# Rotary attention: the causal masks of the score maxima as additions on VectorE instead of products on TensorE

## The chip, the core and the metric

The program runs on one core of one Trainium2 chip. The metric is the device time of one execution in microseconds, as the median of the runs shown. One execution was also recorded by the hardware profiler. The engines are named as in the profile: PE is TensorE (matrix products), PEld its loading of weights, DVE is VectorE, ACT is ScalarE, POOL is GpSimd, SP is SyncE, which issues most transfers. PE writes its products to eight banks of the accumulation memory, called `ps[:, bank, :]` in the code.

## The reference, cut to what matters

The reference is a chain of 16 layers over 8 sequences of 512 tokens with 128 features. One of the layers, `L3_attn_a`, is causal attention with 16 heads whose keys and queries have 8 plain and 32 rotary features each:

```
q = concatenate([q_content, q_rope], -1); k = concatenate([k_content, k_rope], -1)
scores = einsum('bhqd,bhkd->bhqk', q, k) / sqrt(40)
causal = tril(ones((Tx, Tx), bool))
scores = where(causal, scores, -inf)
attn = softmax(scores, -1)
out = einsum('bhqk,bhkd->bhqd', attn, v)
return out.reshape(Bx, Tx, 128) @ W_o
```

## The kernel before

The 16 layers run one after the other as stages, each between barriers of all engines. `rotary_attention` is the stage of `L3_attn_a`. It holds every synchronisation by hand: an engine's instructions run in the order of the code, and semaphores tie the engines together.

The stage computes the scores of a sequence twice. First, with queries on the rows, only to get each query's maximum over the keys (below: the maxima). Then, with keys on the rows (the turned scores), with the negated maximum as an additional row of the product, for the exponential on ACT, whose output is multiplied with the values.

*Maxima.* For a head `n` and a tile `qt` of 128 queries the product is 40 features by 128 queries by `(qt + 1) * 128` keys, so 128, 256, 384 or 512 columns wide (line 908). The last 128 columns are the tile on the diagonal: there, keys later than the query are to be masked. `masked` (line 893) does it on PE: two products of 64 rows each, the two halves of a unit matrix times the two halves of a table of 0 and -1e30, both in bf16, add the table to what is in the bank. DVE then takes the maximum of all columns, negated (line 1057), and its end gives the bank back. Heads come in pairs (`pair_of_maxima`), an even and an odd one; the even head's features lie on rows 0 to 39 and its maxima go to bank 6, the odd head's on rows 64 to 103, bank 7. So PE's two row halves can work on the two heads of a pair at once, and there is one bank for each half's maxima.

*Turned scores.* A pass `u` (16 per sequence) takes one key tile `kt = u % 4` of four heads: two steps of two heads, each with a product of `512 - 128 * kt` columns (line 957) and two mask products per head in banks 0 to 3. ACT takes the exponential (line 1035), and the value products (line 973) follow one pass later.

*What sets the order.* The maxima of sequence 0 are taken first, alone: 32 pairs. In the loop over the passes of sequence `b`, each of the two steps of a pass is followed by one pair of maxima of sequence `b + 1`: passes 0, 2, 4, ... have the widths 128 and 256, passes 1, 3, 5, ... the widths 384 and 512. The last sequence's loop has none. After both steps come the value products of the pass before and then `extras`, side items that use banks 6 and 7 as well: the transposes of the maxima (`turn`, line 915), the projections of sequence `b + 2`, rotary products (lines 932 and 934, taken by DVE in lines 1082 and 1083), sums, context and output of sequence `b - 1`. An item on a bank waits until the item before it on that bank has been taken.

The mask table in bf16 is made by POOL (line 873) once the loads have landed; PE, DVE and SP wait for it at the start of the stage.

Of the kernel before, what the change touches and what calls it, by code (L numbers as in the profile page):

```python
# [11 lines left out]
ALU = mybir.AluOpType  # L12
ACT = mybir.ActivationFunctionType
AX = mybir.AxisListType
F32 = mybir.dt.float32

P = 128
START = 1
BATCH = 8
T = 512  # L20
# [231 lines left out]
KT = T // P  # L252
# [449 lines left out]
def rotary_attention(nc, g, w, d, ks, vaug):  # L702
# [7 lines left out]
    tensors = {"qs": ([P, 2, HALVES, T], F32), "negmax": ([P, KT, NH], F32), "maxrow": ([GH, 2, T], F32),  # L710
               "pt": ([P, 2, KT, T], F32), "o": ([P, 2, T], F32), "sel": ([P, 4, P], F32), "sums": ([P, T], F32), "nope": ([P, 2, T], F32), "prod": ([P, 2, 4, T], F32), "rope": ([P, 2, 2, T], F32),
               "wkv": ([P, 32], F32), "gkv": ([32, 1], F32), "wq": ([P, 64], F32), "wkdec": ([32, P], F32), "wqdec": ([64, P], F32), "wvdec": ([32, P], F32), "wkrope": ([P, 4, P], F32),
               "wqrope": ([64, 4, P], F32), "wo": ([P, P], F32), "cos": ([P, T], F32), "sin": ([P, T], F32), "masks": ([P, 2, 3, P], F32), "masksb": ([P, 2, 3, P], BF16),
               "kvc": ([32, 2, T], F32), "kvsq": ([32, T], F32), "qc": ([64, T], F32), "mean32": ([32, P], F32)}
    loads = [("sel", "sel")] + [(a, "L3a_" + a) for a in ("wkv", "gkv", "wq", "wkdec", "wqdec", "wvdec", "wkrope", "wqrope", "wo", "cos", "sin", "masks")]

# [63 lines left out]
    for item in order():  # L780
# [2 lines left out]
        used[bank] += 1  # L783

    signals = ("loaded pool_ready ready6 ready7 taken6 taken7 squared rooted scaled rope_made nope_written rope_written0 rope_written1 first_stacked second_stacked max_written "
               "max_stacked turned_ready exp_ready pv_done o_copied pool vec")
    with stage(nc, "L3a", tensors, signals) as (block, t, s):
        h, x, ps = g["h"], g["x"], g["ps"]
        nope_d, rope_d, row_d = d["nope"], d["rope"], d["row"]
# [4 lines left out]
        def ready(eng, item):  # L794
            bank, k = place[item]
            eng.wait_ge(s[f"ready{bank}"], START + k + 1)
            return ps[:, bank, :]
# [70 lines left out]
        @block.gpsimd  # L868
        def _(pool):
            own = Chain(pool, s["pool"])  # L870
            own(pool.memset(t["mean32"][:, :], 1.0 / 32))
            pool.wait_ge(s["loaded"], START + LOADED)
            own(pool.tensor_copy(t["masksb"][:, :, :, :], t["masks"][:, :, :, :]), s["pool_ready"], 1)
            for b in range(BATCH):
                for k in range(4):
                    part, half = divmod(k, 2)
                    for ab in range(2):
                        taken(pool, ("rope", b, part, half, ab))

                    pool.wait_ge(s[f"rope_written{k % 2}"], START + (2 * b + k // 2) * 16)  # L880
                    prod = t["prod"][:, k % 2, :, :]
                    pool.tensor_tensor(t["rope"][:, k % 2, 0, :], prod[:, 0, :], prod[:, 3, :], ALU.subtract).then_inc(s["rope_made"], 1)
                    pool.tensor_tensor(t["rope"][:, k % 2, 1, :], prod[:, 2, :], prod[:, 1, :], ALU.add).then_inc(s["rope_made"], 1)

        @block.tensor
        def _(pe):
# [9 lines left out]
            def side(item):  # L896

                bank, k = place[item]
                pe.wait_ge(s[f"taken{bank}"], START + k)
                what, b = item[:2]  # L900
                out = ps[:, bank, :]
                tokens = h[:, b * T:(b + 1) * T]
                if what == "max":
                    n, qt = item[2:]
                    if n % GH == 0 and qt == 0:
                        pe.wait_ge(s["second_stacked" if n else "first_stacked"], START + (b + 1) * STACKED)
                    rows = row_tile(n % 2, KEYED)
                    pe.matmul(out[:, 0:(qt + 1) * P], t["qs"][rows, b % 2, n // 2, qt * P:(qt + 1) * P], ks[rows, b % 2, n // 2, 0:(qt + 1) * P], start=True, stop=False)  # L908
                    mm = masked(out[:, qt * P:(qt + 1) * P], n % 2, 1)
                elif what == "turn":  # L910
                    k = item[2]
                    for r in range(2):
                        taken(pe, ("max", b, GH * k + GH - 2 + r, KT - 1))
                    for qt in range(KT):
                        mm = pe.transpose(out[0:GH, qt * P:(qt + 1) * P], t["negmax"][:, qt, GH * k:GH * (k + 1)], g["ident"][:, :])
                elif what == "kv":
                    mm = pe.matmul(out[0:32, :], t["wkv"][:, :], tokens, start=True, stop=True)
                elif what == "qc":
                    mm = pe.matmul(out[0:64, :], t["wq"][:, :], tokens, start=True, stop=True)
                elif what == "rms":  # L920
                    pe.wait_ge(s["squared"], START + b + 1)
                    mm = pe.matmul(out, t["mean32"][:, :], t["kvsq"][:, :], start=True, stop=True)
                elif what == "qn":
                    taken(pe, ("qc", b))
                    mm = pe.matmul(out, t["wqdec"][:, :], t["qc"][:, :], start=True, stop=True)
                elif what == "kn":
                    pe.wait_ge(s["scaled"], START + b + 1)
                    mm = pe.matmul(out, t["wkdec"][:, :], t["kvc"][:, b % 2, :], start=True, stop=True)
                elif what == "rope":
                    part, half, ab = item[2:]  # L930
                    if part:
                        mm = pe.matmul(out, t["wqrope"][:, 2 * half + ab, :], t["qc"][:, :], start=True, stop=True)
                    else:
                        mm = pe.matmul(out, t["wkrope"][:, 2 * half + ab, :], tokens, start=True, stop=True)
                elif what == "v":
                    pe.wait_ge(s["scaled"], START + b + 1)
                    for kt in range(KT):
                        cols = slice(kt * P, (kt + 1) * P)
                        mm = pe.matmul(out[:, cols], t["kvc"][:, b % 2, cols], t["wvdec"][:, :], start=True, stop=True)
                elif what in ("sums", "ctx"):  # L940
                    pe.wait_ge(s["o_copied"], START + 2 * b + 2)
                    for e in range(2):
                        mm = pe.matmul(out, t["sel"][:, (2 if what == "sums" else 0) + e, :], t["o"][:, e, :], start=(e == 0), stop=(e == 1))
                else:
                    taken(pe, ("ctx", b))
                    mm = pe.matmul(out, t["wo"][:, :], t["sums"][:, :], start=True, stop=True)
                mm.then_inc(s[f"ready{bank}"], 1)
# [97 lines left out]
        def _(vec):  # L1045
# [4 lines left out]
            def maxima(b, i):  # L1050

                for item in pair_of_maxima(b, i):
                    n, qt = item[2:]
                    out = ready(vec, item)
                    if qt == 0 and n % GH == 0 and b:
                        ready(vec, ("turn", b - 1, n // GH))
                    taken_by(vec.tensor_reduce(t["negmax"][:, qt, n:n + 1], out[:, 0:(qt + 1) * P], AX.X, ALU.max, negate=True), item)  # L1057

            def take(item):
# [2651 lines left out]
```

## Time and profile before

| | |
|---|---|
| median of 3 runs | 7737.04 us (7718.37 to 7741.0) |
| profiled execution | 7739.17 us, span 7737.4 us |
| granted clock of PE over the span | 0.83 |
| PE busy | 5852.5 us, 76% of the span |
| DVE busy | 4148.7 us, 54% |
| ACT busy | 2938.2 us, 38% |
| POOL busy | 1964.7 us, 25% |
| rotary stage | about 4131 to 5085 us from the span's start |

Busy time is time in which the engine worked on an instruction; the ends of PE's products are modelled, so a busy PE is not a PE at its peak. The granted clock is the share of PE's full clock that it was given. A product on 32-bit data appears as two records.

### The profile page before, as it was taken

To read this page: it belongs to the slowest core of one execution; us is meant where nothing else is said; L and a number is where in the kernel's file an instruction comes from. 1 tells how busy PE (TensorE), PEld (TensorE's weight loads), DVE (VectorE), ACT (ScalarE), POOL (GpSimd) and SP (SyncE) were. 2 spreads that over 40 slices of the span, in tenths; PEclk is the share of its full clock that TensorE was granted. 3 is DMA by queue.
4 is the path that set the end of the run, shared out by engine and by line. 5 is a ranking of instruction groups with operands and counts; after the bars stand their busy time and mean duration, and the time that the engine had idled before them with its cause. 6 is when DMAs were issued, how large, how long until landed. Compare 5 with 4: busy or idle time off the path is not lost. (4 is left out here: it accounts for less than half of the span.)

```text
span 7737.4 us, 121045 instructions
## 1 busy us (share of the span) xinstructions
PE 5852.5 (76%) x45636; PEld 2850.6 (37%) x45838; DVE 4148.7 (54%) x6437; ACT 2938.2 (38%) x6433; POOL 1964.7 (25%) x1790
## 2 busy tenths in 40 slices
PE   5556667786578876666568999978878889688787
PEld 3445351115352222222223545534434334244343
DVE  4333636662437745778854444445455466555554
ACT  1002223463235541443310222246546455365464
POOL 0004142113142201444422001024234011242341
PEclk6557887897788888787787787889989989899898
DMA  1001022212121100000003122111011000110110
GB/s 46 4 28 56 30 62 75 66 42 69 50 66 39 39 17 14 0 0 0 0 7 62 38 49 54 29 43 45 20 53 45 9 6 0 39 45 23 53 45 20
DMA packets 261164, 269.01 MB, mean 35 GB/s; under 512 B 113600, under 2 KB 190656, under 8 KB 258688
## 3 DMA queue, kind: packets, MB, share of 16 engines
q1 hardware_dynamic: 250368, 240.26, 12.0%
q0 software_dynamic: 10240, 21.25, 0.8%
q8 instruction: 359, 5.88, 0.3%
q14 instruction: 197, 1.61, 0.1%
HBM read 122.59 MB, written 71.66 MB: 25 GB/s over the span
## 5 line engine op out<-in xcount | busy, mean ns | idle before, releaser
L2250 PE MATMUL ps<-s_l2b_hc,ident 128*128 128x512 f32 x512 | 362.4, 848 | 331.0 <-DVE s_l2b_hc L2413 331.0
L2198 POOL TENSOR_TENSOR s_l2b_Bx<-s_l2b_du,s_l2b_B 128x512 f32<-128x512 f32 x256 | 406.5, 1609 | 473.9 <-ACT s_l2b_B L2320 410.8
L1827 PE MATMUL ps<-s_l3l_hs,s_l3l_wqk 128*128 128x512 f32 x512 | 330.9, 754 | 223.5 <-DVE s_l3l_prod L1978 156.5
L1954 ACT ACTIVATE s_l3l_probs<-ps,s_l3l_biases,s_l3l_q_inverse 128x128 f32<-128x128 f32 x1024 | 454.1, 458 | 58.1 <-DVE s_l3l_biases L2024 57.8
L2405 DVE TENSOR_TENSOR_SCAN s_l2b_state<-s_l2b_decay,s_l2b_Bx 128x512 f32<-128x512 f32 x256 | 389.8, 1562 | 155.2 <-ACT s_l2b_decay L2326 113.9
L2022 DVE TENSOR_REDUCE s_l3l_negmax<-ps 128x4 f32<-128x512 f32 x256 | 176.5, 690 | 524.3 <-PE ps L1866 524.3
L1057 DVE TENSOR_REDUCE s_L3a_negmax<-ps 128x1 f32<-128x128 f32 (+3 forms) x512 | 236.3, 488 | 362.9 <-PE ps L893 360.6
L1802 POOL TENSOR_TENSOR s_l3l_probs<-s_l3l_probs,s_l3l_inverse 128x512 f32<-128x512 f32 x256 | 266.6, 1042 | 635.4 <-DVE s_l3l_inverse L2004 633.0
L1035 ACT ACTIVATE s_L3a_pt<-ps 128x256 f32<-128x256 f32 (+3 forms) x512 | 195.2, 434 | 529.3 <-PE ps L893 527.5
L638 DVE TENSOR_REDUCE s_L1a_negmax<-ps 128x1 f32<-128x512 f32 x512 | 316.4, 682 | 139.7 <-PE ps L501 139.3
L908 PE MATMUL ps<-ks,s_L3a_qs 40*128 40x256 f32 (+3 forms) x1024 | 359.8, 610 | 31.3 <-DVE s_L3a_kvsq L1072 16.5
L638 DVE TENSOR_REDUCE s_L2a_negmax<-ps 128x1 f32<-128x512 f32 x512 | 316.7, 682 | 92.1 <-PE ps L501 91.2
L614 ACT ACTIVATE s_L1a_pt<-ps 128x512 f32<-128x512 f32 x512 | 263.1, 603 | 199.2 <-PE ps L537 199.1
L614 ACT ACTIVATE s_L2a_pt<-ps 128x512 f32<-128x512 f32 x512 | 263.3, 604 | 167.0 <-PE ps L537 166.8
L1866 PE MATMUL ps<-s_l3l_qk 64*64 64x64 f32 (+1 forms) x5632 | 281.9, 247 | 42.6 <-issue 24.6
L2250 PEld LDWEIGHTS ps<-s_l2b_hc,ident 128*128 128x128 f32 x512 | 122.0, 257 | 488.9 <-DVE s_l2b_hc L2413 428.6
L957 PE MATMUL ps<-s_L3a_qs,ks 41*128 41x512 f32 (+3 forms) x1024 | 284.2, 567 | 0.1
L1866 PEld LDWEIGHTS ps<-s_l3l_qk 64*64 64x64 f32 x5632 | 218.8, 138 | 161.1 <-issue 161.1
L1948 ACT ACTIVATE s_l3l_turned<-ps 128x512 f32<-128x512 f32 x256 | 152.9, 597 | 316.5 <-PE ps L1874 315.7
L1925 ACT ACTIVATE s_l3l_sq<-ps 128x512 f32<-128x512 f32 x256 | 150.1, 601 | 263.6 <-PE ps L1827 263.6
L501 PE MATMUL ps<-ks,s_L2a_qs 48*128 48x512 bf16 x512 | 177.6, 438 | 85.2 <-DVE s_L2a_negmax L638 37.5
L501 PE MATMUL ps<-ks,s_L1a_qs 48*128 48x512 bf16 x512 | 179.1, 450 | 83.0 <-DMA ks<-scratch_parts 34.7
(663 smaller groups left out, 13292.4 us busy)
## 6 DMA issues: line engine op xcount, KB each, us to landing
s_l3l_qk<-s_l3l_rope SPq DMA_DIRECT2D x1024, 64.0 KB
scratch_rope<-s_L3a_rope SPq DMA_DIRECT2D x32, 512.0 KB, 2.8
ks<-scratch_parts SPq DMA_DIRECT2D x384, 32.0 KB
s_L3a_qs<-scratch_rope SPq DMA_DIRECT2D x64, 128.0 KB
ks<-scratch_rope SPq DMA_DIRECT2D x64, 128.0 KB
s_L0e_slots<-scratch_sent SPq DMA_DIRECT2D x16, 396.0 KB, 5.6
s_L1e_slots<-scratch_sent SPq DMA_DIRECT2D x16, 396.0 KB, 6.0
scratch_square<-s_L1a_rows SPq DMA_DIRECT2D x24, 256.0 KB, 3.0
```

Source lines behind the costliest of these rows:

```text
L501: mm = pe.matmul(out, t["qs"][rows, b % 2, n // 2, qt * P:(qt + 1) * P], ks[rows, b % 2, n // 2, :], start=True, stop=True)
L614: act.activation(t["pt"][:, u % 2, j, :], ps[:, j, :], ACT.Exp, scale=scale).then_inc(s["exp_ready"], 1)
L638: taken_by(vec.tensor_reduce(t["negmax"][:, qt, n:n + 1], out, AX.X, ALU.max, negate=True), item)
L908: pe.matmul(out[:, 0:(qt + 1) * P], t["qs"][rows, b % 2, n // 2, qt * P:(qt + 1) * P], ks[rows, b % 2, n // 2, 0:(qt + 1) * P], start=True ...
L957: pe.matmul(ps[:, 2 * pair + r, first(kt):T], ks[rows, b % 2, 2 * four + pair, kt * P:(kt + 1) * P], t["qs"][rows, b % 2, 2 * four + pair, ...
L1802: own(pool.tensor_tensor(tile, tile, share, ALU.mult), s["probs_ready"], U + 1)
L1827: mm = pe.matmul(out, t["wqk"][:, 2 * e + ab, :], tokens, start=True, stop=True)
L1866: mm = pe.matmul(out[rows, P * k + at:P * k + at + size], t["qk"][rows, b % 2, c, 64 * m:64 * m + 64], t["qk"][rows, b % 2, 4 + c, key:key ...
L1954: act.activation(t["probs"][:, U % (LAG + 1), k, :], ps[:, U % 2, P * k:P * (k + 1)], ACT.Exp, bias=t["biases"][:, U % (LAG + 1), k:k + 1] ...
L2198: pool.tensor_tensor(t["Bx"][:, n % 2, k, :], t["du"][:, b % 2, k, :], t["B"][:, n % 2, :], ALU.mult).then_inc(s["bx_ready"], 1)
L2250: pe.matmul(ps[:, 4 + k, :], g["ident"][:, :], t["hc"][:, n % 2, k, :], start=(n == 0), stop=(n == STATES - 1)).then_inc(s["summed"], 1)
L2405: vec.tensor_tensor_scan(t["state"][:, k, :], t["decay"][:, n % 2, k, :], t["Bx"][:, n % 2, k, :], 0.0, ALU.mult, ALU.add).then_inc(s["sca ...
```

## The change

The two mask products of each head's maxima are left out; the score product alone fills the bank. DVE instead adds a mask tile of 128 by 128 in 32 bits to the last 128 columns, in the bank, waits for that addition with a semaphore of its own (`masked`), and then takes the maximum as before. The tile is made on POOL at the start of the stage by a fill and a cut along the diagonal. The turned scores keep their mask products.

```diff
-               ... "masksb": ([P, 2, 3, P], BF16),
+               ... "masksb": ([P, 2, 3, P], BF16), "mask": ([P, P], F32),
...
             own(pool.memset(t["mean32"][:, :], 1.0 / 32))
+            own(pool.memset(t["mask"][:, :], 0.0))
+            own(pool.affine_select(out=t["mask"][:, :], in_=t["mask"][:, :], compare_op=ALU.is_ge, fill=-1e30, base=0, pattern=[[-1, P]], channel_multiplier=1))
             pool.wait_ge(s["loaded"], START + LOADED)
...
                     rows = row_tile(n % 2, KEYED)
-                    pe.matmul(out[:, 0:(qt + 1) * P], t["qs"][rows, b % 2, n // 2, qt * P:(qt + 1) * P], ks[rows, b % 2, n // 2, 0:(qt + 1) * P], start=True, stop=False)
-                    mm = masked(out[:, qt * P:(qt + 1) * P], n % 2, 1)
+                    mm = pe.matmul(out[:, 0:(qt + 1) * P], t["qs"][rows, b % 2, n // 2, qt * P:(qt + 1) * P], ks[rows, b % 2, n // 2, 0:(qt + 1) * P], start=True, stop=True)
...
                         ready(vec, ("turn", b - 1, n // GH))
+                    last = out[:, qt * P:(qt + 1) * P]
+                    vec.tensor_tensor(last, last, t["mask"][:, :], ALU.add).then_inc(s["masked"], 1)
+                    vec.wait_ge(s["masked"], START + NH * KT * b + 2 * i + n % 2 + 1)
                     taken_by(vec.tensor_reduce(t["negmax"][:, qt, n:n + 1], out[:, 0:(qt + 1) * P], AX.X, ALU.max, negate=True), item)
```

On PE, an odd pass with 128-wide turned scores read thus before; each row is an instruction with its output and inputs and the size of its output, `xN` is how often it stands there:

```order
L957 MATMUL ps<-s_L3a_qs,ks 128x128 x2
L893 MATMUL ps<-s_L3a_masksb 128x128 x4
L908 MATMUL ps<-ks,s_L3a_qs 128x384
L893 MATMUL ps<-s_L3a_masksb 128x128 x2
L908 MATMUL ps<-ks,s_L3a_qs 128x384
L893 MATMUL ps<-s_L3a_masksb 128x128 x2
L957 MATMUL ps<-s_L3a_qs,ks 128x128 x2
L893 MATMUL ps<-s_L3a_masksb 128x128 x4
L908 MATMUL ps<-ks,s_L3a_qs 128x512
L893 MATMUL ps<-s_L3a_masksb 128x128 x2
L908 MATMUL ps<-ks,s_L3a_qs 128x512
L893 MATMUL ps<-s_L3a_masksb 128x128 x2
```

The same pass of the changed kernel, whose lines have other numbers (957 is 958, 893 is 895, 908 is 910):

```order
L958 MATMUL ps<-s_L3a_qs,ks 128x128 x2
L895 MATMUL ps<-s_L3a_masksb 128x128 x4
L910 MATMUL ps<-ks,s_L3a_qs 128x384 x2
L958 MATMUL ps<-s_L3a_qs,ks 128x128 x2
L895 MATMUL ps<-s_L3a_masksb 128x128 x4
L910 MATMUL ps<-ks,s_L3a_qs 128x512 x2
```

The two heads' products now follow each other directly, and only the turned scores' mask products remain. On DVE, between the copy of the values and the reciprocal of the sums (pass 4), four reduces stood before:

```order
L1088 COPY vaug<-ps 128x64x8
L1057 TENSOR_REDUCE s_L3a_negmax<-ps 128x1 x4
L1093 RECIPROCAL s_L3a_sums<-ps 128x512
L1097 TENSOR_TENSOR s_L3a_sums<-s_L3a_sums,ps 128x512
L1057 TENSOR_REDUCE s_L3a_negmax<-ps 128x1 x8
```

Now, in the changed kernel:

```order
L1092 COPY vaug<-ps 128x64x8
L1059 TENSOR_TENSOR ps<-ps,s_L3a_mask 128x128
L1061 TENSOR_REDUCE s_L3a_negmax<-ps 128x1
L1059 TENSOR_TENSOR ps<-ps,s_L3a_mask 128x128
L1061 TENSOR_REDUCE s_L3a_negmax<-ps 128x1
L1059 TENSOR_TENSOR ps<-ps,s_L3a_mask 128x128
L1061 TENSOR_REDUCE s_L3a_negmax<-ps 128x1
L1059 TENSOR_TENSOR ps<-ps,s_L3a_mask 128x128
L1061 TENSOR_REDUCE s_L3a_negmax<-ps 128x1
L1097 RECIPROCAL s_L3a_sums<-ps 128x512
```

Each reduce has an addition ahead of it, even head and odd head in turn, and the reciprocal stands behind four of each.

## Rows read from the trace of the kernel before

**Rows 1.** The page, its first line: the span.

```profile
span 7737.4 us, 121045 instructions
```

**Rows 2.** Windows of the stage: length, busy PE PEld DVE ACT POOL, PEclk, DMA share, GB/s.

```profile
4192.00:4267.00 75.00, 72.74 (x260) 42.94 (x262) 33.38 (x69) 1.87 (x2) 6.25 (x6) 0.52 0.42 78
4267.00:4376.00 109.00, 105.21 (x693) 57.88 (x691) 47.37 (x88) 31.03 (x73) 9.97 (x8) 0.77 0.17 39
4598.80:4710.30 111.50, 106.29 (x716) 55.44 (x716) 52.11 (x92) 31.35 (x75) 9.96 (x8) 0.83 0.26 51
```

**Rows 3.** Waits in the stage, 4185 to 5100 us: total us, times, longest.

```profile
DVE s_L3a_negmax L1057 <- PE ps L893: 360.6, 294, 4.7
PEld ps L893 <- issue: 159.6, 485, 0.7
...
PEld ps L915 <- DVE s_L3a_negmax L1057: 15.3, 14, 1.7
PEld ps L908 <- DVE s_L3a_negmax L1057: 15.3, 62, 0.5
```

**Rows 4.** Timeline of PE in three places: start, length, instruction, [idle before <- releaser].

```profile
4430.70 0.29 PE L893 MATMUL ps<-s_L3a_masksb 64*128 64x128 bf16 x4
4430.81 0.66 PE L957 MATMUL ps<-s_L3a_qs,ks 41*128 41x256 f32 x4
4431.30 0.29 PE L893 MATMUL ps<-s_L3a_masksb 64*128 64x128 bf16 x4
4431.41 0.84 PE L908 MATMUL ps<-ks,s_L3a_qs 40*128 40x256 f32 x4
...
4688.76 0.48 PE L893 MATMUL ps<-s_L3a_masksb 64*128 64x128 bf16 x4
4688.97 2.08 PE L957 MATMUL ps<-s_L3a_qs,ks 41*128 41x512 f32 x4
4690.78 0.48 PE L893 MATMUL ps<-s_L3a_masksb 64*128 64x128 bf16 x4
...
4707.35 0.33 PE L893 MATMUL ps<-s_L3a_masksb 64*128 64x128 bf16 x4
4707.89 1.16 PE L908 MATMUL ps<-ks,s_L3a_qs 40*128 40x512 f32 x3 [0.21 <-DVE s_L3a_negmax L1057]
```

**Rows 5.** Timeline of DVE in three places.

```profile
4431.01 0.49 DVE L1057 TENSOR_REDUCE s_L3a_negmax<-ps 128x1 f32<-128x128 f32 x2 [2.64 <-PE ps L893]
...
4610.96 0.68 DVE L1067 COPY s_L3a_kvc<-ps 32x512 f32<-32x512 f32 x1 [1.68 <-PE ps L917]
4611.68 0.68 DVE L1069 TENSOR_TENSOR s_L3a_kvsq<-s_L3a_kvc 32x512 f32<-32x512 f32 x1
...
4707.27 1.02 DVE L1057 TENSOR_REDUCE s_L3a_negmax<-ps 128x1 f32<-128x384 f32 x2 [1.56 <-PE ps L893]
```

**Rows 6.** One group of the stage: count, busy us, mean ns, idle before.

```profile
L893 PE MATMUL ps<-s_L3a_masksb 64*128 64x128 bf16 x2048 | 233.2, 248 | 0.0
```

**Rows 7.** Single lines of other stages: duration in ns, least, median, most.

```profile
L2767 DVE TENSOR_TENSOR s_L1e_steps<-s_L1e_prefix,s_L1e_steps x2: 293/293/293, 1801.7 to 2091.9; 128x128 f32<-128x128 f32 x2
...
L2496 DVE TENSOR_TENSOR s_L2r_hot<-s_L2r_hot,s_L2r_order x4: 424/425/426, 2868.9 to 3992.0; 128x256 f32<-128x256 f32 x4
...
L1368 DVE TENSOR_TENSOR s_l0a_NT<-ps,s_l0a_masks x16: 424/424/425, 102.8 to 464.4; 128x256 f32<-128x256 f32 x16
```

**Rows 8.** Timeline in the first maxima, a 512-wide pair: PE, then DVE.

```profile
4258.17 1.16 PE L893 MATMUL ps<-s_L3a_masksb 64*128 64x128 bf16 x4
4258.63 1.43 DVE L1057 TENSOR_REDUCE s_L3a_negmax<-ps 128x1 f32<-128x512 f32 x2 [1.64 <-PE ps L893]
```

**Rows 9.** Timeline of POOL at the start of the stage.

```profile
4141.59 0.82 POOL L873 CAST s_L3a_masksb<-s_L3a_masks 128x768 bf16<-128x768 f32 x1 [9.96 <-DMA s_L3a_masks<-in_L3a_masks_dram]
```

**Rows 10.** Passes 11 to 14 of sequences 6 and 5, columns as in rows 2.

```profile
4913.71:4930.77 17.06, 16.88 (x160) 9.59 (x161) 8.37 (x18) 5.98 (x16) 2.48 (x2) 1.00 0.51 92
4789.14:4817.74 28.60, 28.43 (x161) 14.35 (x161) 8.36 (x18) 5.97 (x16) 2.49 (x2) 0.55 0.41 66
```

More of the change, by code:

```diff
@@ L712, in rotary_attention @@
                "wkv": ([P, 32], F32), "gkv": ([32, 1], F32), "wq": ([P, 64], F32), "wkdec": ([32, P], F32), "wqdec": ([64, P], F32), "wvdec": ([32, P], F32), "wkrope": ([P, 4, P], F32),
-               "wqrope": ([64, 4, P], F32), "wo": ([P, P], F32), "cos": ([P, T], F32), "sin": ([P, T], F32), "masks": ([P, 2, 3, P], F32), "masksb": ([P, 2, 3, P], BF16),
+               "wqrope": ([64, 4, P], F32), "wo": ([P, P], F32), "cos": ([P, T], F32), "sin": ([P, T], F32), "masks": ([P, 2, 3, P], F32), "masksb": ([P, 2, 3, P], BF16), "mask": ([P, P], F32),
                "kvc": ([32, 2, T], F32), "kvsq": ([32, T], F32), "qc": ([64, T], F32), "mean32": ([32, P], F32)}
@@ L785, in rotary_attention @@
     signals = ("loaded pool_ready ready6 ready7 taken6 taken7 squared rooted scaled rope_made nope_written rope_written0 rope_written1 first_stacked second_stacked max_written "
-               "max_stacked turned_ready exp_ready pv_done o_copied pool vec")
+               "max_stacked masked turned_ready exp_ready pv_done o_copied pool vec")
     with stage(nc, "L3a", tensors, signals) as (block, t, s):
```

## The prediction

> **What bounds the kernel now.** I read the views from the whole to the place. The page gives the span [rows 1]. The windows of the rotary stage come next [rows 2]: in every stretch TensorE (PE) is busy for about 96% of the time and VectorE (DVE) for under half, so PE looks like the bound; the column PEclk says that it gets 0.52 of its full clock while the maxima of sequence 0 are taken alone, 0.77 to 0.83 in the loops over passes. Its clock has two levels, 1.2 and 2.4 GHz, so 0.83 is two thirds of the time at the upper one. Then the waits [rows 3]: DVE waits 360.6 us in all for the products of the maxima. The other direction is small, 15.3 us in 62 waits of PE's weight loads for the reduce. It is small because PE's two row halves (even head, odd head) overlap: while one waits, the other counts as busy. Whether DVE already sets the pace must be read from the timeline, pair by pair.
>
> There [rows 4, 5], upper clock, pass 2 of a sequence: the masks of a pair start at 4430.70 and the next scores at 4430.81, so four mask products hold PE 0.11 us. The two reduces start at 4431.01, 0.31 us after the masks, and last 0.49 us together, until 4431.50. The second pair of maxima begins at 4431.41: its even head fits in, its odd head needs the bank that is free only at 4431.50. So here there is no slack between DVE and PE at all. In pass 15 it is plainer: the scores' masks begin at 4707.35, yet the next pair starts at 4707.89 after an idle 0.21 us that the row puts down to the reduce; the first of the two 384-wide reduces (1.02 us for both, from 4707.27) ends at about 4707.8. At the lower clock mask products hold PE 0.21 us (4688.76 to 4688.97), and the 512-wide scores behind them 1.81 us (to 4690.78): there PE is slow enough that DVE is mostly done in time.
>
> So of the four second pairs in four passes, three are released by DVE at the upper clock; the first pairs come after value products and a new pass's scores, and DVE was idle before them, 2.64 us ahead of the reduces of 4431.01. That is where the additions land.
>
> **The change part by part.** *Removed from PE:* four of the eight mask products per score-and-maxima step. In the loops there are 7 sequences of 32 pairs, 224 pairs. Two thirds at 0.11 and one third at 0.21 us [rows 4] give 224 x 0.145 = 33 us. This is the lower end of the gain: all 2048 mask products together are busy 233.2 us [rows 6], of which half, 117 us, is the upper end. I take 33, because the start-to-start times show what PE really gives up and the busy time counts pipelined ends.
>
> *Added to DVE:* per head one addition of 128 columns and a wait on itself. The trace has no addition that writes a bank. The nearest row is 128x128 in SBUF, 0.293 us; at 256 columns an addition or product with an operand in the bank takes 0.424 us and one all in SBUF 0.425 us [rows 7], so the bank costs nothing extra when read, and I take 0.293. The self-wait costs 0.04 us: the copy of line 1067 starts at 4610.96 and lasts 0.68, the instruction that waits for it starts at 4611.68 [rows 5]. Together D = 0.33 us per head. Bounds: below, 0.21 us, what a second 128-wide reduce adds to its row (0.49 for two, the first 0.28); above, 0.424 + 0.04 = 0.46 us.
>
> The Trainium skill, Perfetto Trace Analysis, section Optimizing Scalar/DVE Operations, speaks against this choice: it gives DVE an access overhead of about 60 ns on SBUF and 125 ns on PSUM, the latency in a profile being about twice that. By it an addition in the bank would take some 0.42 us as an estimate, D 0.46, and the sum below 30 us more; the rows on bank operands do not agree for reads, and no row shows a write.
>
> *Where D falls on the path.* The odd head's bank is released after two additions and two reduces, 2D = 0.66 us later when both heads are ready together, D when the odd head is itself late by more than D. PE's own part is earlier by the masks, which is counted already. Of each second pair there are 28 (7 sequences, 4 four-pass groups), 19 at the upper clock by two thirds.
> - Scores 256 wide between (passes 2, 6, ...): no slack at the upper clock, 19 x 0.66; at the lower the scores take twice as long, 0.4 us of slack, 9 x 0.27. Sum 15 us.
> - Scores 512 wide between (passes 0, 4, ...): at the upper clock they last 0.42 us more than 256-wide ones (0.90, half of 1.81, against the 0.49 from 4430.81 to the masks of 4431.30), less the 0.14 by which the odd head is late above: slack 0.28, 19 x 0.38 = 7 us. Nothing at the lower clock.
> - The 512-wide maxima of odd passes (384- or 128-wide scores ahead): released by DVE now, as in pass 15; 0.66 where the heads are in step, 0.33 where the odd one is late. I take 0.5 for all 56: 28 us.
>
> Together 50 us of waits. *Behind them:* what is queued behind the waiting reduce on DVE are the side items' products and copies, and the side items on PE need the same two banks. The transposes of the maxima wait for the reduce 14 times already [rows 3]; those, the sums of pass 4 and two rotary products per sequence find little slack. Some 20 starts later by D: 6 us.
>
> *The first maxima* (sequence 0, lower clock) are a chain per bank: product, masks, reduce, next product [rows 8], the reduce 0.46 us after the masks began. Each of 32 items per bank loses 0.21 of masks and gains 0.33: 32 x 0.12 = 4 us.
>
> *GpSimd* fills and cuts the mask tile, two instructions on 128 columns, in the 9.96 us in which it waits for the masks' load; its cast of 768 columns behind that takes 0.82 us [rows 9], so the two cost nothing, and without that cover at most 2 x 0.82 us.
>
> Sum with the clock as it is: 50 + 6 + 4 - 33 = +27 us.
>
> *The clock.* The same four passes (11 to 14) took 17.06 us at a granted 1.00 in sequence 6 and 28.60 us at 0.55 in sequence 5 [rows 10]: about 2.9 us per pass at the lower level. In the first stretch of rows 2, where PE alternates with DVE, the clock stayed low, in the loops it is high two thirds of the time. After the change PE has fewer columns and longer waits, so the same direction. I take five more low passes of 112, +15 us; this is a choice, bounded by nothing worse than rival 1 and by 0 on the other side.
>
> Forecast +42 us. The profiled execution took 7739.17 us (span 7737.4), 2 us over the median of the three runs, 7737.04; so 7737 + 42, 7779 us, with 7760 to 7815 as its own range.
>
> **The rivals.**
> 1. *The clock falls for much longer.* If one more group of four passes per sequence runs low, 7 x 11.5 = 80 us on top of 27: about 7845 us. For it: the first maxima ran low throughout. Against: at the lower clock the waits on DVE vanish and PE is dense again, after which it rose each time. The Trainium skill, TensorE: Matmul & The Clock Gate, section on a second failure mode (cycling through PSUM banks), says that short idle times between matmul groups make the clock swing; the trace agrees in so far as the clock changes in these loops, and by that rule this rival is the outcome.
> 2. *No change.* If the addition costs its lower bound, D 0.21, the same three terms give 8 + 3 + 17 = 28 us, behind them 4, the first maxima 0, the masks -33: 7736 us. For it: in a queue without waits the end of one DVE instruction overlaps the start of the next. Against: this addition is waited for by the very next instruction.
> 3. *Faster.* The mask products cost PE more than their start-to-start time, since each also needs its weights loaded. At the upper end of 117 us the sum is 50 + 6 + 4 - 117 = -57: 7680 us. The point from which it decides is 0.27 us saved per pair (60 over 224). For it: 159.6 us of idle on the load path ahead of mask loads [rows 3]. Against: in the rows the next matmul starts 0.11 us after the masks, no later.
>
> **How the numbers follow.** Measurable from no change is here about 0.3%, 23 us. Forecast 0.47, rival 1 0.18, rival 2 0.20, rival 3 0.15. So faster 0.15, same 0.20, slower 0.65. The range takes in rival 2, most of rival 1 and the part of rival 3 that a saving of some 0.35 us per pair would give, 7718; left out are its far end and a clock low in most passes, together under 2 in 10: 7718 to 7845.
>
> **What would show it.** Right: the additions take 0.27 to 0.32 us and the reduce follows 0.04 us later; the waits of PE's weight loads for the reduce of the maxima, 15.3 us before [rows 3], grow several fold; the stage lengthens by 30 to 60 us, and outside it nothing moves by more than a few. The 256-wide second pairs start their odd head about 0.5 us later after the even one. Wrong: additions under 0.25 us, a second pair that starts right behind the scores, or a granted clock in the loops that moves by over 0.05 either way, which outweighs the waits.

## The result and the profile after

The changed kernel takes 7815.62 us (median of 4 runs, 7810.0 to 7830.81); the kernel before 7732.91 (median of 4, 7718.37 to 7741.0). The ratio is 1.0112, 95% interval 1.0096 to 1.0127: slower by about 83 us. The forecast was slower by 42 us, 7779, with a range to 7845. The direction and the range held; the size is twice the forecast, and it has to be found where the other half came from. The profiled execution took 7810.0 us, that of the kernel before 7739.17. Each trace is one execution, so the traces differ by 71 us where the medians differ by 83. On its page the span answers to [rows 1]:

```profile
span 7808.3 us, 119513 instructions
## 1 busy us (share of the span) xinstructions
PE 5921.6 (76%) x44612; PEld 2817.6 (36%) x44814; DVE 4295.0 (55%) x6949; ACT 2940.3 (38%) x6433; POOL 1964.3 (25%) x1792
```

The additions are one line of DVE. The view of that line gives their duration (least, median, most, in ns), and the timeline of DVE shows them in a pass of the same kind as in the first part of [rows 5], at the upper clock:

```profile
L1059 DVE TENSOR_TENSOR ps<-ps,s_L3a_mask x512: 287/299/300, 4205.4 to 5108.3; 128x128 f32<-128x128 f32 x171
```

```profile
5017.62 0.30 DVE L1059 TENSOR_TENSOR ps<-ps,s_L3a_mask 128x128 f32<-128x128 f32 x1 [2.46 <-PE ps L910]
5017.95 0.29 DVE L1061 TENSOR_REDUCE s_L3a_negmax<-ps 128x1 f32<-128x128 f32 x1
5018.16 0.29 DVE L1059 TENSOR_TENSOR ps<-ps,s_L3a_mask 128x128 f32<-128x128 f32 x1
5018.48 0.29 DVE L1061 TENSOR_REDUCE s_L3a_negmax<-ps 128x1 f32<-128x128 f32 x1
```

An addition lasts 0.30 us and its reduce starts 0.03 us behind it. So the even head's bank is free at 5018.24 and the odd head's at 5018.77, and the next product of PE waits for each: the two heads' products start at 5018.30 and 5018.83, 0.53 us apart. The waits of the stage, 4185 to 5170 us, in rows that answer to [rows 3] (lines 908, 915, 1057 of before are 910, 916, 1061 here):

```profile
DVE ps L1059 <- PE ps L910: 276.4, 248, 4.3
...
PEld ps L895 <- issue: 92.1, 215, 0.7
...
PEld ps L910 <- DVE s_L3a_negmax L1061: 79.9, 150, 1.9
...
PEld ps L916 <- DVE s_L3a_negmax L1061: 22.2, 15, 2.8
```

The weight loads of the maxima (line 908, now 910) waited 15.3 us in 62 waits for the reduces and now wait 79.9 us in 150.

Where the time went is read from windows with equal marks: a pass begins with its first product of maxima. First the kernel before, in the columns of [rows 2]: the whole stage; sequences 1 to 6 of the loops; then sequence 4 in its pieces (passes 0 and 1, 2 to 4, 5 to 10, 11 to 14, 15); last, one pass with 256-wide scores and no side item at the upper and at the lower clock.

```profile
4131.40:5080.50 949.10, 886.03 (x5536) 458.37 (x5536) 406.00 (x711) 244.66 (x581) 80.68 (x66) 0.77 0.24 48
4269.32:4937.41 668.09, 636.10 (x4147) 332.29 (x4144) 299.04 (x531) 187.95 (x440) 59.77 (x48) 0.80 0.24 47
4602.27:4612.51 10.24, 10.24 (x86) 5.46 (x81) 4.92 (x10) 5.04 (x10) 0.00 (x0) 1.00 0.75 91
4612.51:4641.86 29.35, 25.86 (x147) 13.90 (x141) 12.93 (x16) 8.97 (x19) 0.00 (x0) 0.71 0.03 10
4641.86:4680.05 38.19, 36.85 (x265) 18.99 (x265) 21.40 (x41) 10.28 (x27) 7.48 (x6) 1.00 0.13 49
4680.05:4706.26 26.21, 26.04 (x160) 13.14 (x161) 8.36 (x18) 5.97 (x16) 2.49 (x2) 0.61 0.46 72
4706.26:4711.39 5.13, 4.92 (x55) 2.74 (x50) 3.00 (x5) 0.89 (x4) 0.00 (x0) 1.00 0.35 79
4927.68:4930.77 3.09, 3.09 (x46) 2.17 (x41) 1.25 (x4) 1.32 (x4) 0.00 (x0) 1.00 1.09 102
4812.21:4817.74 5.53, 5.53 (x45) 3.53 (x41) 1.24 (x4) 1.32 (x4) 0.00 (x0) 0.50 0.00 1
```

The same windows of the changed kernel, with the first maxima as the second row:

```profile
4140.90:5163.50 1022.60, 951.65 (x4512) 427.85 (x4512) 556.19 (x1224) 244.78 (x581) 81.11 (x68) 0.71 0.22 44
4204.35:4282.33 77.98, 73.72 (x138) 33.29 (x140) 50.32 (x130) 1.87 (x2) 4.93 (x4) 0.50 0.40 72
4282.33:5003.35 721.02, 685.11 (x3380) 312.31 (x3378) 412.19 (x916) 186.92 (x438) 59.71 (x48) 0.73 0.22 44
4645.06:4660.78 15.72, 15.72 (x68) 7.52 (x65) 7.31 (x18) 5.04 (x10) 0.00 (x0) 0.58 0.34 42
4660.78:4691.36 30.58, 28.19 (x123) 13.19 (x117) 16.53 (x28) 8.46 (x18) 0.00 (x0) 0.61 0.03 10
4691.36:4730.95 39.59, 37.35 (x217) 16.81 (x217) 28.23 (x65) 10.81 (x28) 7.47 (x6) 1.00 0.13 47
4730.95:4757.10 26.15, 25.70 (x128) 11.10 (x130) 13.14 (x34) 5.97 (x16) 2.48 (x2) 0.61 0.43 72
4757.10:4764.48 7.38, 6.74 (x47) 2.81 (x42) 4.24 (x9) 0.89 (x4) 0.00 (x0) 0.74 0.55 104
5017.14:5020.68 3.54, 3.47 (x39) 2.06 (x34) 2.44 (x8) 1.32 (x4) 0.00 (x0) 1.00 0.04 8
5097.33:5102.71 5.38, 5.38 (x37) 3.07 (x34) 2.44 (x8) 1.31 (x4) 0.00 (x0) 0.50 0.00 0
```

Read them in this order. The stage is 73.5 us longer, while the span grew by 70.9. Outside the stage the code is the same, and there the traces differ both ways: the stage starts 9.5 us later and the part behind it is 12.1 us shorter. Over all traces of this case the stage starts between 4120 and 4145 us, so some ten us outside the stage are no effect of the change. Of the stage's 73.5 us sequences 1 to 6 hold 52.9, everything from the maxima of sequence 7 to the end of the stage 17.1 (143.1 to 160.2 us), the first maxima 3.4 (74.6 to 78.0); ahead of them the stage took 63.4 and 63.5 us. Within sequence 4, passes 5 to 10 ran at 1.00 both times and cost 1.40 us more; passes 11 to 14 ran at 0.61 both times and cost 0.06 less. Ten of sixteen passes together: +1.3 us. Passes 0 and 1, whose clock went from 1.00 to 0.58, cost 5.48 more, and pass 15, from 1.00 to 0.74, 2.25 more. So three passes whose clock changed hold 7.7 of the sequence's 10.3 us, and passes 2 to 4, at 0.71 before and 0.61 now, 1.2. The pattern repeats: sequences 3 to 6 of the changed kernel take 119.41, 119.42, 119.43 and 119.44 us, with nearly the same clocks in the same passes. So a pass that is pushed to the lower clock can cost its price once in every sequence.

### The profile page after: what moved, and what is told of

It is laid out like the page before. It is cut to its first block and busy times, and to the rows that moved or that the text cites. A ratio compares the mean times of both kernels' runs of the same rounds, so it can differ in the third digit from the quotient of the medians.

```text
span 7808.3 us, 119513 instructions
## 1 busy us (share of the span) xinstructions
PE 5921.6 (76%) x44612; PEld 2817.6 (36%) x44814; DVE 4295.0 (55%) x6949; ACT 2940.3 (38%) x6433; POOL 1964.3 (25%) x1792
## 5 line engine op out<-in xcount | busy, mean ns | idle before, releaser
L910 PE MATMUL ps<-ks,s_L3a_qs 40*128 40x128 f32 (+3 forms) x1024 | 408.5, 661 | 35.0 <-DVE s_L3a_kvsq L1076 13.0
L1059 DVE TENSOR_TENSOR ps<-ps,s_L3a_mask 128x128 f32<-128x128 f32 x512 | 151.4, 296 | 279.8 <-PE ps L910 276.4
L958 PE MATMUL ps<-s_L3a_qs,ks 41*128 41x512 f32 (+3 forms) x1024 | 302.7, 615 | 0.0
L501 PE MATMUL ps<-ks,s_L1a_qs 48*128 48x512 bf16 x512 | 182.0, 457 | 80.6 <-DMA ks<-scratch_parts 33.7
```

Source lines behind the costliest of these rows:

```text
L910: mm = pe.matmul(out[:, 0:(qt + 1) * P], t["qs"][rows, b % 2, n // 2, qt * P:(qt + 1) * P], ks[rows, b % 2, n // 2, 0:(qt + 1) * P], start ...
L958: pe.matmul(ps[:, 2 * pair + r, first(kt):T], ks[rows, b % 2, 2 * four + pair, kt * P:(kt + 1) * P], t["qs"][rows, b % 2, 2 * four + pair, ...
```

## The experiments

**The two theories.** The theory of the sum: the loss is waits of PE for the additions, less the mask products. The theory of the clock: most of it is the granted clock of PE, which falls in other places than before. The expectations of the first runs split it in two: by the waits theory the clock follows PE's waits for DVE, by the columns theory it follows how many products PE has. Loops are sequences 1 to 6, from the first maxima product of sequence 1 to that of sequence 7; the kernel before is 668.1 us at 0.80, the changed one 721.0 at 0.73. The kernels ran in three groups; the kernel before took 7726.13, 7722.23 and 7733.01 us in them (medians of 17, 17 and 18 runs), and each ratio is against its own group.

**Masks on neither engine, and on both.** These two and the two kernels of the case make a square: mask products of the maxima or none, additions or none. The first run leaves the masks of the maxima out (its exponent is scaled down so that it stays finite, and its output is not the layer's):

```diff
-                    last = out[:, qt * P:(qt + 1) * P]
-                    vec.tensor_tensor(last, last, t["mask"][:, :], ALU.add).then_inc(s["masked"], 1)
-                    vec.wait_ge(s["masked"], START + NH * KT * b + 2 * i + n % 2 + 1)
...
```

> The maxima get no mask at all, neither on PE nor on DVE, and the exponent is scaled down by 1000 so that no sum vanishes; the output is therefore not the layer's. It prices the removal of 1024 mask products alone. Waits theory (the clock fell in the changed kernel because PE waits longer for DVE): no added wait, so the clock in the loops stays at 0.78 to 0.83 and the 33 us of the loops and 7 us of the first maxima come off: about 7690 us. Columns theory (the clock fell because PE has four products fewer per step): the clock falls to about 0.74 here too, and the time is 7720 to 7745 us.

The second puts the mask products of the maxima back beside the additions:

```diff
-  mm = pe.matmul(out[:, 0:(qt + 1) * P], ..., start=True, stop=True)
+  pe.matmul(out[:, 0:(qt + 1) * P], ..., start=True, stop=False)
+  mm = masked(out[:, qt * P:(qt + 1) * P], n % 2, 1)
```

> The changed kernel with the mask products of the maxima put back, so that each mask is added twice, by PE and by DVE. PE has all products of before, DVE all additions of after. Waits theory: the clock falls as in the changed kernel, loops at about 0.74, and the time is that of after plus the 33 us and 7 us of mask products: 7845 to 7860 us. Columns theory: the clock is that of before, 0.82, and only the waits of 50 + 6 and 11 us in the first maxima are added: about 7800 us.

Without masks 7723.65 us, ratio 0.9998 (0.9985 to 1.0011); with both 7879.71, ratio 1.0196 (1.0182 to 1.0211). Windows of the loops and of the pass kind shown last above, upper clock, then lower, first for the kernel without masks, then for the one with both:

```profile
4269.61:4945.58 675.97, 639.38 (x3379) 292.22 (x3377) 298.28 (x531) 187.02 (x438) 59.73 (x48) 0.75 0.23 47
5013.92:5016.78 2.86, 2.86 (x38) 1.75 (x34) 1.24 (x4) 1.32 (x4) 0.00 (x0) 1.00 0.00 0
4813.41:4818.35 4.94, 4.94 (x37) 2.63 (x34) 1.24 (x4) 1.32 (x4) 0.00 (x0) 0.50 0.05 7
```

```profile
4292.75:5067.98 775.23, 741.10 (x4149) 380.16 (x4145) 412.70 (x916) 186.96 (x438) 59.80 (x48) 0.70 0.20 41
5108.02:5111.78 3.76, 3.70 (x46) 2.42 (x41) 2.44 (x8) 1.32 (x4) 0.00 (x0) 1.00 0.00 0
4926.83:4932.63 5.80, 5.80 (x45) 3.77 (x41) 2.44 (x8) 1.32 (x4) 0.00 (x0) 0.50 0.00 1
```

At one clock level the pass is a sum, plain at the upper level and to within 0.17 us at the lower. Upper level: the additions cost 0.67 us with masks (3.09 to 3.76) and 0.68 without (2.86 to 3.54); the mask products cost 0.23 without additions and 0.22 with them. Lower level: additions 0.27 with masks (5.53 to 5.80) and 0.44 without; masks 0.59 and 0.42. The whole is no such sum. Taking the masks away saves nothing where there are no additions (0.9998) and about 0.85% where there are (1.0196 against 1.0112). The kernel without masks is faster than the one before at both levels, yet its loops are 8 us longer, because the clock gave 0.75 instead of 0.80. That is the theory of the clock, in a kernel that has no added instruction at all. It doesn't have unchanged waits, though: without the mask products PE comes to the banks earlier and waits longer for the same reduces, 43.4 us in 92 waits against 15.3 in 62 [rows 3]:

```profile
PEld ps L908 <- DVE s_L3a_negmax L1056: 43.4, 92, 1.6
```

So the first run, whose time and clock are about those that the columns theory gave, doesn't separate missing columns from longer waits. The second came out above both forecasts, at 0.70 with all products of before; by the columns theory its clock would have stayed.

**One half of the additions.** Tiles 0 and 2 are the first pairs of a pass, tiles 1 and 3 the second ones; the other half keeps its mask products.

```diff
+                    if qt % 2 == 0:        # second run: == 1
                         last = out[:, qt * P:(qt + 1) * P]
...
```

> DVE adds the mask only for the first pair of each pass (query tiles 0 and 2); the second pair (tiles 1 and 3) keeps its mask products. My steps: the release of the first pair's banks is what the second pair waits for, so nearly all 50 us of waits are here, with half of the mask saving, 16 us. Waits theory: clock about 0.75 in the loops, 7800 to 7830 us. Columns theory: half the columns are gone, clock between, about 7780 us.

> The other half: DVE adds the mask only for the second pair of each pass (tiles 1 and 3), whose banks are needed only a pass later; the first pair keeps its mask products. My steps: nearly no wait but the side items' 6 us, half of the mask saving, 16 us: 7715 to 7735 us, clock as before. Columns theory: the same columns are gone as in the run on the first pairs, so the same clock as there, about 7760 to 7780 us.

First pairs: 7830.76 us, ratio 1.0144 (1.0129 to 1.0158), loops 740.6 us at 0.72. Second pairs: 7766.49, ratio 1.0047 (1.0033 to 1.006). At one clock the additions that hurt are those of a first pair, since the second pair of its pass waits for the banks; behind a second pair come value products and a new pass, with time to spare. Passes 5 to 10 show it, at the upper clock throughout: 38.19 us before, 39.74 with additions on first pairs, 38.00 on second pairs. Windows: these passes in sequence 2 of the first run; then of the second run its loops, the same passes in sequence 3, and the pass kind that took 3.09 us before, upper clock:

```profile
4440.10:4479.84 39.74, 37.91 (x241) 18.57 (x241) 24.90 (x53) 10.79 (x28) 7.47 (x6) 1.00 0.13 47
```

```profile
4269.52:4989.59 720.07, 688.99 (x3765) 332.28 (x3761) 354.00 (x724) 186.88 (x438) 59.73 (x48) 0.72 0.21 44
4555.53:4593.53 38.00, 36.31 (x240) 17.49 (x241) 24.65 (x53) 10.24 (x27) 7.47 (x6) 1.00 0.13 49
5055.73:5058.71 2.98, 2.98 (x42) 1.95 (x37) 1.72 (x6) 1.32 (x4) 0.00 (x0) 1.00 0.00 0
```

On second pairs the pass is 0.11 us shorter than before, the loops 52 us longer, at 0.72: in the loops the loss is nearly all clock. (The rest of its stage ran at 0.99 and gave part back.) The expectation of 7715 to 7735 us missed by over 30: its sum held in passes 5 to 10, but not its clock. The time and the clock, the same 0.72 as on first pairs, are those of the columns theory; on first pairs the time was within 1 us of the range of the waits theory. Neither theory fits all four runs.

**Giving PE work back.** If the missing columns lowered the clock, more of them should raise it; so says the density theory of the expectations, by which waits and missing products both lower the clock. Three kernels: the changed one with each mask product of the turned scores done twice; the changed one with the 128-wide turned scores done three times and the 256-wide ones twice, in the wait ahead of the second pair; the kernel before with the 128-wide ones done twice.

```diff
-                for j in range(2):
+                for j in range(4):                                           # the first
+  again = (0, 0, 1, 2)[kt] if pair and b + 1 < BATCH else 0                  # the second; (0, 0, 0, 1) the third
+  for k in range(again + 1):
       for r in range(2):
...
```

> The changed kernel with the turned scores' mask products done twice (the masked scores only become more negative): PE has as many products as before, but none of the added ones between the maxima and DVE. Density theory (the clock falls both when PE waits and when it has fewer products): PE is denser than in after, the clock in the loops rises from 0.73 to 0.76 or more, which gives back part of the 40 us that the products cost: 7815 to 7845 us. Rival (the clock follows the waits alone): 0.72 or less and 7855 us or more.

> The changed kernel with products that change nothing put where PE waits for DVE: ahead of the second pair of maxima the turned score product is done two more times where it is 128 wide and once more where it is 256 wide (the last one counts). Density theory: they run in time that was idle, PE stays denser and the clock in the loops rises to 0.78 or more: 7770 to 7800 us, faster than after with more work. Rival (only the waits for DVE count, the clock is a symptom): not faster than 7810 us, and up to 7840 us if the products do not fit into the waits.

> The kernel before with the same filler in its one plain wait: ahead of the second pair of maxima the 128-wide turned score product is done once more. Density theory: clock in the loops 0.82 or more instead of 0.80, 7700 to 7720 us, faster than before. Rival: the work adds to the path or is hidden, 7727 to 7740 us.

7809.87 us (ratio 1.0115, 1.0099 to 1.0131), 7792.82 (1.0096, 1.0081 to 1.0111) and 7722.41 (1.0006, 0.9995 to 1.0016). The first has 768 matmuls more in its loops than the changed kernel and takes the same time (1.0115 against 1.0112, 5 us under the forecast range), its loops 708.8 us at 0.77: there the work is paid by a higher clock. The other two don't bear the theory out. The second has a time in the forecast range, but its loops ran at 0.73, not at the 0.78 expected, and took 727.4 us; its interval overlaps that of the changed kernel. The third ran at 0.79 in loops of 675.5 us, against 0.80 and 668.1, and is as fast as the kernel before, where 0.82 or more and a gain were expected. So one of three fillers raised the clock, and neither of the two for the changed kernel brings it near the one before.

**One addition for both heads.** 256 columns, after both products, then the two reduces:

```diff
+                last = ps[:, 6:8, qt * P:(qt + 1) * P]
+                vec.tensor_tensor(last, last, both, ALU.add).then_inc(s["masked"], 1)
...
```

> The changed kernel with one addition of 2 x 128 columns for both heads of a pair (about 0.42 us, as the 256-wide rows) in place of two of 0.296 with a wait each. The odd head's bank comes free 0.2 us earlier, the even one's 0.13 us later. By my steps the waits of the second pairs shrink by about 0.2 us each where the heads are in step: 10 to 15 us at the same clock, 7800 to 7806 us; if the clock follows the waits it rises by 0.01 to 0.02 and another 10 to 20 us come off: 7780 to 7795 us. Rival (the odd head's release is not what the loops wait for): 7815 us or more.

7953.95 us, ratio 1.0301 (1.0286 to 1.0316): the expectation missed by some 150 us. The view of the line, then windows of the first maxima, of the loops, and of the known pass kind at the upper and at the lower clock:

```profile
L1061 DVE TENSOR_TENSOR ps<-ps,s_L3a_mask x256: 431/433/433, 4198.6 to 5258.2; 128x256 f32<-128x256 f32 x128
```

```profile
4196.47:4293.55 97.08, 61.08 (x138) 30.00 (x140) 42.87 (x98) 1.87 (x2) 4.93 (x4) 0.50 0.32 58
4293.55:5145.78 852.23, 795.04 (x3379) 360.65 (x3377) 379.37 (x724) 187.21 (x438) 59.71 (x48) 0.59 0.19 37
5189.92:5193.71 3.79, 3.42 (x38) 2.04 (x33) 2.22 (x7) 1.32 (x4) 0.00 (x0) 1.00 0.00 0
5247.43:5252.72 5.29, 5.29 (x37) 2.83 (x34) 2.11 (x6) 1.32 (x4) 0.00 (x0) 0.50 0.00 0
```

DVE is indeed busy for less (379 against 412 us in the loops). But now the even head waits for the odd one, no product of the next pair starts before both, and the pass takes 3.79 instead of 3.54 us at the upper clock; at the lower one it takes 5.29 instead of 5.38. In the first maxima, low in both kernels, the lock costs 19 us (97.1 against 78.0). In the loops 0.25 us for each of 96 passes would be 24 us; they lost 131, at a clock of 0.59. An estimate from these rows: 852.23 us at 0.59 and 721.02 at 0.73 are about 699 and 389 us at the lower level, and 310 us more there, at 5.29 for 3.79, cost some 88. So most of this loss too came with the clock. The expectation reckoned with the addition alone.

**One wait, in one place.** Ahead of the products of the maxima no wait of PE itself for a reduce is longer, in the changed kernel, than the 0.64 us in pass 15, where it waited 0.21 us before [rows 4]; in sequence 4 the clock falls about 1.6 us after that row begins, and stays low until pass 1 of the next sequence. Timeline of PE:

```profile
4758.95 2.08 PE L910 MATMUL ps<-ks,s_L3a_qs 40*128 40x512 f32 x4 [0.64 <-DVE s_L3a_negmax L1061]
```

Is it this wait that makes it fall? Four kernels choose the engine by a rule; the first is the changed kernel with pass 15's 384-wide maxima masked by PE, the second its mirror, the third has all 384-wide maxima on PE, the fourth is a control with the 14 additions in pass 7:

```diff
+    def added(b, n, qt):
+        return b == 0 or n < NH - 2 or qt != 2         # 1
+        return b > 0 and n >= NH - 2 and qt == 2       # 2
+        return qt != 2                                 # 3
+        return b > 0 and n // 2 == 3 and qt == 2       # 4
...
```

> The changed kernel, with only the 384-wide maxima of pass 15 of each looped sequence masked by TensorE as before (56 of 512 additions fewer... exactly 14: two heads, seven sequences). In the changed kernel TensorE stands idle 0.64 us there (before 0.21), and the granted clock falls about 1.6 us later and stays low until pass 1 of the next sequence. Theory A, that this one wait makes it fall: passes 15, 0 and 1 run at the upper level again in most sequences, the loops of sequences 1 to 6 come from 721 us to 675 to 695, the whole to 7765 to 7790 us. Theory B, that the clock answers to all waits and to the missing mask products together, or falls elsewhere: within 6 us of the changed kernel, 7805 to 7820 us.

> The mirror of the run above: every mask by TensorE as in the kernel before, and the addition on VectorE only for the 384-wide maxima of pass 15 of each looped sequence, 14 additions in all. At the same clock it costs at most 7 x 0.45 us, 3 us. Theory A (this wait makes the clock fall for passes 15 to 1): 7745 to 7775 us. Theory B (no single wait does it): 7722 to 7735 us, no difference that can be measured.

> The changed kernel, with all 384-wide maxima (query tile 2, the first pair of every odd pass) masked by TensorE, the other three tiles by additions on VectorE. The waits of the 512-wide second pairs in odd passes go back to those of the kernel before, so that at the same clock the loops lose about 15 us against the changed kernel. Theory A (the long waits ahead of the 512-wide maxima make the clock fall): 7740 to 7775 us. Theory B (the clock answers to all of it): 7780 to 7805 us.

> A control for the run with additions in pass 15 alone: the same 14 additions, but on the 384-wide maxima of pass 7, in a stretch (passes 5 to 10) where both kernels keep the upper clock. Theory A (the place decides, pass 15 is on the edge): 7722 to 7735 us, no difference. Theory B (no single wait does it): the same. A third theory, that any one wait more makes the clock fall: 7745 to 7775 us.

Windows of the first: its loops, passes 0 and 1 of sequences 4 and 5.

```profile
4271.47:4996.97 725.50, 693.40 (x3405) 316.31 (x3402) 408.49 (x904) 186.90 (x438) 59.74 (x48) 0.72 0.21 43
4640.93:4656.69 15.76, 15.76 (x68) 7.55 (x65) 7.31 (x18) 5.04 (x10) 0.00 (x0) 0.58 0.43 43
4758.04:4769.01 10.97, 10.71 (x70) 4.73 (x65) 7.64 (x19) 5.04 (x10) 0.00 (x0) 1.00 0.76 89
```

It takes 7815.94 us (ratio 1.0107, 1.0085 to 1.0129), as the changed kernel does: theory B of its expectation. (The count in it is 14 additions, two heads in seven sequences.) The wait is back at 0.20 us, and in sequences 5 and 7 passes 0 and 1 do run at the upper clock, but then passes 6 and 7 or others run low: the low stretch moved. Theory A, that this one wait sets the changed kernel's time, is refuted. The row of sequence 5 also prices the change in passes 0 and 1 at one clock: 10.97 against 10.24 us.

The mirror takes 7767.72 us, ratio 1.0052 (1.0032 to 1.0071), 35 us for 14 additions. Its trace is its fastest execution, 7744.35 us. Windows: loops, pass 15 of sequence 4, passes 0 and 1 behind it.

```profile
4267.62:4958.00 690.38, 657.09 (x4123) 336.61 (x4120) 303.30 (x543) 186.91 (x438) 59.81 (x48) 0.77 0.23 46
4721.74:4729.13 7.39, 6.75 (x51) 3.11 (x45) 3.70 (x7) 0.89 (x4) 0.00 (x0) 0.75 0.59 100
4729.13:4745.37 16.24, 16.24 (x85) 7.66 (x81) 4.92 (x10) 5.05 (x10) 0.00 (x0) 0.59 0.37 38
```

Here theory A's range holds: the clock falls in pass 15 and passes 0 and 1 cost 16.24 instead of 10.24 us. But in sequences 3 and 5 of the same trace pass 15 ran at 1.00, and the passes 0 and 1 behind it were low all the same (16.33 and 16.37 us at 0.58). So the range is borne out and theory A's path only in part. The third kernel takes 7801.49 us, ratio 1.0078 (1.0054 to 1.0102), in theory B's range; its loops, expected to be some 15 us shorter than those of the changed kernel at the same clock, are 14 us longer, 734.6 us at 0.70. The control takes 7714.01 us, ratio 0.9975 (0.9964 to 0.9987), which none of its three theories had. Its windows, as for the mirror:

```profile
4270.80:4931.32 660.52, 629.86 (x4123) 329.49 (x4120) 302.45 (x543) 186.99 (x438) 59.75 (x48) 0.81 0.24 48
4707.78:4712.90 5.12, 4.92 (x55) 2.73 (x49) 3.00 (x5) 0.89 (x4) 0.00 (x0) 1.00 0.33 75
4712.90:4723.14 10.24, 10.24 (x86) 5.47 (x81) 4.91 (x10) 5.04 (x10) 0.00 (x0) 1.00 0.84 94
```

In its trace every sequence from the second on takes 109.1 to 109.2 us, with passes 0 and 1 at 1.00, where those of the kernel before took 109, 111 or 115. So the same 14 additions cost 35 us in one pass and gain 19 in another. Of the runs here it is the one that beats both kernels, by 0.25%, less than the 0.3% that the prediction took as measurable, though the interval leaves 1 out. Why a wait in pass 7 keeps the clock in step is not settled, so it is no recipe.

## Why the prediction was right or wrong

**The price of an addition: right.** 0.296 us as a mean and 0.03 to the reduce, D = 0.33 as taken from [rows 5, 7]; an addition in the bank takes no longer than the SBUF row of 0.293. The estimate worked out from the Trainium skill, Perfetto Trace Analysis, section Optimizing Scalar/DVE Operations, 0.42 us, does not hold in this trace: the longest of 512 additions took 0.300 us.

**Where D falls: right.** For a second pair behind 256-wide scores the sum said 0.66 us at the upper and 0.27 at the lower clock; the square measured 0.67 and 0.68, and 0.27 (0.44 without mask products). Eight mask products in a pass, 0.22 and 0.42 by [rows 4], were 0.22 to 0.23 and 0.42 to 0.59. So the pass should lose 0.44 at the upper clock and gain 0.15 at the lower, and it lost 0.45 (3.09 to 3.54) and gained 0.15 (5.53 to 5.38). The heads' products start 0.53 us apart, where the prediction had about 0.5. For odd passes the sum was too high: 0.5 of waits less 0.22 of masks is 0.28 us a pass, and passes 5 and 7 of sequence 4, at 1.00 in both traces, grew by 0.11 each (6.43 to 6.54 and 7.60 to 7.71).

**The first maxima: right.** 4 us, measured 3.4. GpSimd's share at nothing is right: from the start of the stage to the first maxima the traces take 63.4 and 63.5 us. The waits of PE's loads grew fivefold, as said.

**The sum at one clock, +27 us: right within what can be told.** In sequence 4, 1.40 (passes 5 to 10) and -0.06 (11 to 14) are measured at equal clocks, and so is 0.73 for passes 0 and 1, with the run that masked pass 15 on PE; for passes 2 to 4 and 15 I estimate 1 us from the 0.45 of the one pass kind. That is about 3 us for a sequence, 21 for seven, 24 with the first maxima.

**The clock: the term that was too small.** The prediction took "five more low passes of 112, +15 us; this is a choice". Its direction was right. By the line above, 73.5 - 24, about 50 us of the stage are the clock's, more than three times as much. An estimate by another way agrees: by its rows, 949.10 us at 0.77 and 1022.60 at 0.71, the stage spent about 437 and then 593 us at the lower level, some 157 more; the known pass kind takes 5.38 us there and 3.54 at the upper level, so 157 us there cost some 54. Passes 0 and 1 ran wholly at the upper clock in sequences 3, 4 and 5 before and in none after; passes 11 to 14 of sequence 6 did so before, 17.06 us [rows 10], and took 26.19 us at 0.61 after. This is the mechanism of rival 1, which had one more group of four passes low in every sequence, 80 us and 7845 in all; the result lies between, at 7816, and nearer to the rival than to the forecast. It is at the end of the forecast's own range (7815); the full range held because most of rival 1 was taken in. The prediction also named, as a sign that it was wrong, a clock in the loops that moves by more than 0.05 and outweighs the waits: it moved by 0.07. And the stage grew by 73.5 us, not by 30 to 60. The reason against rival 1, that at the lower clock PE is dense and the clock comes back, says nothing on when it falls again.

**What moves the clock.** Shown: it fell when additions came with the same PE work (0.80 to 0.70), and when mask products went and nothing was added (0.80 to 0.75). In the second case PE's waits for the reduces grew as well, 15.3 to 43.4 us. The Trainium skill, TensorE: Matmul & The Clock Gate, section A second HAM failure mode, names short idle times between groups of matmuls as what makes the clock swing; the growth of the waits in the kernel without masks agrees with it. Not shown is whether missing products alone, at unchanged waits, lower the clock. Not shown either is where it will fall: a wait in pass 15 goes with a lower clock in one kernel and, taken out of another, only moves the fall. That cause stays open.

**Rivals 2 and 3.** An addition at the lower bound is refuted by its row. That masks cost more than their start-to-start time is true by a little at the lower clock (0.59 against 0.42 where no addition is made). Per pair that is 0.11 us at the upper clock and 0.21 to 0.30 at the lower, and the rival needed 0.27 on average. In the whole time the kernel without any mask shows that even all of them, with no addition in their place, returned nothing.

## What to carry to other kernels

Where TensorE's granted clock is a mix of its two levels, price a change pass by pass at each level, and keep the clock as a term of its own, as wide as the passes near the edge between the levels; here it was some 50 of the 73.5 us by which the stage grew. Work taken from TensorE in such a loop may give nothing back, and a gain in a pass can end as a loss: with additions on second pairs alone passes 5 to 10 were 0.19 us shorter at the upper clock, and the whole was 0.47% longer. So a change is to be read in the whole time and not in a pass. When one of two alternating pairs has slack behind it, additional work costs less there: at the upper clock additions on second pairs did not lengthen passes 5 to 10, those on first pairs did, by 1.55 us.

## What the runs showed that was not expected

- Fourteen additions, 4 us of DVE's time in all, changed the whole by +35 us in pass 15 and by -19 us in pass 7.
- 768 more matmuls in the loops (the mask products of the turned scores twice) left the time as it was, 7809.87 against 7815.62 us (ratios 1.0115 and 1.0112), at a clock of 0.77 instead of 0.73.
- The kernel without masks has 768 matmuls less in its loops than the kernel before (3379 against 4147) and takes the same time, 7723.65 against 7726.13 us.
- An addition of 256 columns in the bank took 0.433 us against 2 x 0.296 for two of 128, and the kernel with it lost some 140 us against the one with two. It ties the two heads together, which cost 19 us in the first maxima at one clock; most of the rest came with a clock of 0.59 in the loops.
